# Half a tile more distance between the scores and what reads the probabilities back

## The reference, cut to what matters

```python
Q, K, V = (proj(Wq), proj(Wk), proj(Wv))
scores = jnp.einsum('bhqd,bhkd->bhqk', Q, K) / SCALE
idx = clip(k - q, -MAX_LEN, MAX_LEN) + MAX_LEN
scores = scores + jnp.einsum('bhqd,qkd->bhqk', Q, pek[idx]) / SCALE
scores = jnp.where(causal, scores, -jnp.inf)
attn = jax.nn.softmax(scores, axis=-1)
out = einsum('bhqk,bhkd->bhqd', attn, V) + einsum('bhqk,qkd->bhqd', attn, pev[idx])
x = _layernorm(x + out @ Wo.T)
x = _layernorm(x + (silu(x @ wg.T) * (x @ wu.T)) @ wd.T)
```

## Time and profile before

| | us |
|---|---|
| median of 3 runs | 5945.27 (5935.37 to 5958.6) |
| the profiled execution | 5937.08 |
| its span | 5935.4 |

### The profile page before, as it was taken

How to read it: one execution, slowest core, us unless ns; L and a number is a source line. 1 busy time by engine, 2 the same in 40 slices (tenths; PEclk the granted TensorE clock), 3 DMA queues, 4 the chain that set the end, 5 groups by cost and what they waited for, 6 DMA issues and landing times. The chain is left out here.

```text
span 5935.4 us, 143051 instructions
## 1 busy us (share of the span) xinstructions
PE 5156.7 (87%) x49460; PEld 3407.6 (57%) x49460; DVE 3809.4 (64%) x8777; ACT 3447.7 (58%) x7512; POOL 1838.5 (31%) x2516
## 2 busy tenths in 40 slices
PE   9977888888888888888888888888888799999999
PEld 5545555555555555555555555555555556666655
DVE  5546676676667766676667666776677645555554
ACT  4436777777777777777777777777677511111111
POOL 4443333333333333333333333333333211111111
PEclk9989999999999999999999999999999999999999
DMA  7888999999999999899999999899999711111111
GB/s 225 253 225 278 287 299 292 285 294 297 287 290 294 302 292 298 286 292 295 294 290 294 290 293 291 289 296 296 283 293 291 248 54 57 57 57 57 57 57 39
DMA packets 653784, 1417.28 MB, mean 239 GB/s; under 512 B 64004, under 2 KB 362088, under 8 KB 640872
## 3 DMA queue, kind: packets, MB, share of 16 engines
q1 hardware_dynamic: 653160, 1409.10, 75.7%
HBM read 737.46 MB, written 671.35 MB: 237 GB/s over the span
## 5 line engine op out<-in xcount | busy, mean ns | idle before, releaser
L791 ACT ACTIVATE a_prob<-a_neg_s,a_neg_max 128x384 f32<-128x384 f32 (+1 forms) x1792 | 1076.1, 601 | 275.1 <-DVE a_neg_max L840 255.8
L511 DVE COPY a_p_t<-a_t_ps 128x512 f32<-128x512 f32 (+3 forms) x1536 | 954.3, 621 | 258.5 <-PE a_t_ps L755 251.9
L688 PE MATMUL a_s_ps<-a_k,a_q 96*128 96x512 bf16 (+3 forms) x3072 | 860.1, 334 | 192.8 <-ACT a_far L795 178.2
L762 PE MATMUL a_t_ps<-a_ident,a_band 128*128 128x128 f32 x3840 | 630.6, 285 | 384.3 <-DMA a_band<-prob_scr 359.4
L798 ACT ACTIVATE a_b_out<-a_t_ps 128x512 f32<-128x512 f32 (+1 forms) x1024 | 582.2, 569 | 635.9 <-PE a_t_ps L698 632.7
L840 DVE CUSTOM_DVE_ANT_1 a_neg_s<-a_s_ps,a_bias,a_far_neg 128x384 f32<-128x384 f32 x1280 | 791.1, 618 | 237.3 <-DVE a_far_neg L834 237.3
L755 PE MATMUL a_t_ps<-a_ident,a_prob 128*128 128x128 f32 x5120 | 865.4, 276 | 0.2 <-DVE a_p_t L511 0.2
L834 DVE TENSOR_REDUCE a_far_neg<-a_s_ps 128x1 f32<-128x640 f32 (+4 forms) x1280 | 708.9, 554 | 220.5 <-PE a_s_ps L688 120.9
L716 PE MATMUL a_o_ps<-a_p_t,a_v 128*32 128x128 f32 x18432 | 832.1, 294 | 0.2 <-ACT a_o_t L803 0.2
L798 ACT ACTIVATE a_p_t<-a_t_ps 128x512 f32<-128x512 f32 (+3 forms) x1536 | 669.7, 436 | 155.2 <-PE a_t_ps L755 151.4
L795 ACT ACTIVATE a_far<-a_s_ps,a_neg_max 128x640 f32<-128x640 f32 (+4 forms) x1280 | 732.4, 572 | 0.0
(11 more groups left out here) (99 smaller groups left out, 6660.9 us busy)
## 6 DMA issues: line engine op xcount, KB each, us to landing
a_bias<-bias_scr SPq DMA_DIRECT2D x448, 576.0 KB, 6.2
prob_scr<-a_prob SPq DMA_DIRECT2D x448, 576.0 KB, 7.1
bias_scr<-a_b_out SPq DMA_DIRECT2D x448, 512.0 KB, 4.0
a_band<-prob_scr SPq DMA_DIRECT2D x448, 512.0 KB, 6.1
qk_scr<-p_parts SPq DMA_DIRECT2D x256, 192.0 KB, 3.4
v_scr<-p_v_out SPq DMA_DIRECT2D x256, 128.0 KB, 2.2
a_v<-v_scr SPq DMA_DIRECT2D x64, 512.0 KB, 7.0
attn_scr<-a_o_t SPq DMA_DIRECT2D x512, 64.0 KB, 6.4
```

Of the source, the lines that this page charges most:

```text
L511: copy(p_t[par][:, u, blocks[0] * P:(blocks[-1] + 1) * P], bank[:, 0:len(blocks) * P]) \
L688: mm = pe.matmul(s_ps[:, u % 2, c:e], q_s[0:ROWS, g, u, qb * P:(qb + 1) * P], k_s[0:ROWS, g, u, c:e], start=True, stop=True)
L762: mm = pe.transpose(bank[:, n * P:(n + 1) * P], band_block(kk, 2 * i + n // 2, n % 2), ident[:, :])
L791: e = act.activation(near_prob(k, u, near(qb)), neg_s[:, u % 2, 0:w].rearrange("p (b c) -> p b c", c=P), ACT.Exp, bias=neg_max[:, u:u + 1] ...
```

## The change

The transposes of the probabilities run six units behind the scores in place of four: in unit u of step k PE takes head (u - 6) mod 4 of tile k - 2 (units 0 and 1: heads 2 and 3) or k - 1 (units 2 and 3: heads 0 and 1). The band transposes, the three parts of the values and the relative values all run two units later as well, and ACT's copy to `o_t` with them. SP stores a tile's result a step later (in step k+4) and always waits for ACT's copy first. The loop has one more step at its very end.

```diff
-    DEPTH = 4
+    DEPTH = 5
...
-        BAND_SLOTS = ((3, 2), (0, 3))
-        VALUE_SLOTS = ((2, 2), (3, 2), (0, 3))
-        REL_SLOT = (1, 3)
+        P_LAG = 6
+        BAND_SLOTS = ((1, 3), (2, 3))
+        VALUE_SLOTS = ((0, 3), (1, 3), (2, 3))
+        REL_SLOT = (3, 3)
...
-                if ok(k - 1):
-                    jobs += [("p", u, k - 1, i) for i in range(len(t_banks(q_block(k - 1))))]
+                kp, head = k + (u - P_LAG) // GRP, (u - P_LAG) % GRP
+                if ok(kp):
+                    jobs += [("p", u, kp, i, head) for i in range(len(t_banks(q_block(kp))))]
...
-                    if k >= 0 and ok(k - 3):
-                        par = (k - 3) % 2
-                        qb, g = q_block(k - 3), ((k - 3) % TILES) // QB
-
-                        if not ok(k + LEAD):
-                            sp.wait_ge(o_evac, T - 2)
-                        row = attn[r_prev if k < 3 else r]
+                    if k >= 0 and ok(k - 4):
+                        par = k % 2
+                        qb, g = q_block(k - 4), ((k - 4) % TILES) // QB
+
+                        sp.wait_ge(o_evac, T - 3)
+                        row = attn[r_prev if k < 4 else r]
                         sp.dma_start(row[g, :, qb * P:(qb + 1) * P], o_t[:, par]).then_inc(stored[par], 16)
...
-                                pe.wait_ge(exp_ready, 4 * (TILES * r + kk) + u + 1)
+                                pe.wait_ge(exp_ready, 4 * (TILES * r + kk) + head + 1)
...
-                        if (u, 3) == REL_SLOT and ok(k - 3) and k >= 0:
+                        if u == REL_SLOT[0] and ok(k - 3) and k >= 0:
                             relative(r, k - 3)
...
-                        if u == 1 and ok(k - 3) and k >= 0:
+                        if u == REL_SLOT[0] and ok(k - 3) and k >= 0:
                             act.wait_ge(o_mm, T - 2)
                             if ok(k - 5):
                                 act.wait_ge(stored[(k - 3) % 2], pair(r, k - 5))
```

More of the change, by code:

```diff
@@ L462, in plan @@
                 if ok(k + LEAD) and u in BIAS_SLOTS:
-                    jobs.append(("bias", u, k + LEAD, BIAS_SLOTS.index(u)))
-                if ok(k - 1):
-                    jobs += [("p", u, k - 1, i) for i in range(len(t_banks(q_block(k - 1))))]
+                    jobs.append(("bias", u, k + LEAD, BIAS_SLOTS.index(u), None))
+                kp, head = k + (u - P_LAG) // GRP, (u - P_LAG) % GRP
+                if ok(kp):
+                    jobs += [("p", u, kp, i, head) for i in range(len(t_banks(q_block(kp))))]
                 for i, (at, back) in enumerate(BAND_SLOTS):
                     if u == at and ok(k - back):
-                        jobs.append(("band", u, k - back, i))
+                        jobs.append(("band", u, k - back, i, None))
             return jobs
@@ L480, in wait_evac @@
         def wait_evac(eng, r, job):
-            kind, u, kk, i = job
+            kind, _, kk, i, head = job
             if kind == "band":
@@ L485, in wait_evac @@
             elif kind == "p":
-                who = t_engine(q_block(kk), u, i)
-                eng.wait_ge(t_evac[who], t_done(who, r, kk, u, i))
+                who = t_engine(q_block(kk), head, i)
+                eng.wait_ge(t_evac[who], t_done(who, r, kk, head, i))
             else:
@@ L499, in read_out @@
         def read_out(eng, copy, name, r, k, u, first, last):
-            for pos, (kind, uu, kk, i) in enumerate(plan(k, first, last)):
+            for pos, (kind, uu, kk, i, head) in enumerate(plan(k, first, last)):
                 if uu != u:
@@ L505, in read_out @@
                 by_head = bank.rearrange("p (h j) -> p h j", h=2)[:, :, j:]
-                if kind == "p" and t_engine(q_block(kk), u, i) == name:
+                if kind == "p" and t_engine(q_block(kk), head, i) == name:
                     blocks = t_banks(q_block(kk))[i]
-                    eng.wait_ge(t_mm, t_made(r, kk, u) - len(t_banks(q_block(kk))) + i + 1)
+                    eng.wait_ge(t_mm, t_made(r, kk, head) - len(t_banks(q_block(kk))) + i + 1)
                     if valid(kk - 2, first, last):
                         eng.wait_ge(pv_mm, TILES * r + kk - 1)
-                    copy(p_t[par][:, u, blocks[0] * P:(blocks[-1] + 1) * P], bank[:, 0:len(blocks) * P]) \
+                    copy(p_t[par][:, head, blocks[0] * P:(blocks[-1] + 1) * P], bank[:, 0:len(blocks) * P]) \
                         .then_inc(t_evac[name], 1)
@@ L742, in body @@
                         for pos, job in enumerate(jobs):
-                            kind, uu, kk, i = job
+                            kind, uu, kk, i, head = job
                             if uu != u:
@@ L752, in body @@
                             elif kind == "p":
-                                pe.wait_ge(exp_ready, 4 * (TILES * r + kk) + u + 1)
+                                pe.wait_ge(exp_ready, 4 * (TILES * r + kk) + head + 1)
                                 for n, b in enumerate(t_banks(q_block(kk))[i]):
                                     mm = pe.transpose(bank[:, n * P:(n + 1) * P],
-                                                      prob_block(kk, u, b), ident[:, :])
+                                                      prob_block(kk, head, b), ident[:, :])
                                 mm.then_inc(t_mm, 1)
```

## The result

| | before | changed |
|---|---|---|
| median of the runs | 5951.9 us (4 runs) | 5699.5 us (4 runs: 5692.3 to 5712.8) |
| ratio | 1 | 0.957 (95% interval 0.9551 to 0.9589) |
| span of the profiled execution | 5935.4 us | 5690.6 us |

The changed kernel takes 252 us less. The forecast was 5800 us with a range of 5670 to 5930, so the direction and the range hold, and the gain was taken too small (141 us). The time is nearer to that of rival A (5670 us) than to that of the forecast.

A forecast was written before the change was run, and what follows sets the result against it. Nothing full, PE 85% and DMA 93% busy; PE's band wait held back stores and loads. Per round 2.7 - 0.4 - 0.1 = 2.2 us, x 64 = 141; 5937.1 - 141 + 3 gave 5800 us, range 5670 to 5930.

The forecast's parts named there:

- rival A: Attention stage: nearly all comes back, DMA runs full, new store wait does not show; 4.2 us a round, 5670 us; chance 0.20.
- The bands: PE's wait for the `a_band` load before band transposes goes altogether; gain at most 5.6 us a round, or 358 us.
- What comes back: Part of the band wait regained per round, limited by DMA: between 0 and 4.7 us, taken as 2.7 us.
- floor: Round length at a full DMA share of 1.00: 66.6 x 0.93 = 61.9 us, a gain of 4.7 us.
- The relative-key chain: `a_bias` load and POOL's selects before DVE: 7.7 us, up to 10.1; holds the DMA share at 0.97.
- The store: ACT's copy of a result tile waits for an earlier store to land: 0 to 1.9 us a round, taken as 0.4.
- The banks: A step's last transposes and the next relative keys share a bank; PE waits for ACT's copy, 0.1 us a round.
- The copies: DVE's heavy copies gather around heavy steps: 2.8 to 4.4 us a round, mostly hidden, taken as 0.
- rival C: DVE's heavy copies beside heavy steps are paid in full, 2.8 to 4.4 us a round; slower, 5995 us; chance 0.11.
- B: Band wait turns into DVE and ACT waits for `a_bias`; round shrinks within 0.3 us, 5918 to 5940 us; chance 0.12.
- D: Band transposes still wait, as SP's load comes later by its new wait; 5.6 us stay, 5935 us; chance 0.05.

The follow-up runs named there:

- e1: Kernel before, but PE's band transposes read a constant tile and wait for no load (relative values left out of the result): 5723.5 us, ratio 0.9604.
- e9: Kernel before, band transposes of a constant tile (relative values left out), three `a_bias` buffers and their earlier load: 5473.8 us, ratio 0.918.
- e4: Changed kernel, but POOL masks a constant tile without waiting for `a_bias` (relative-key scores left out of the result): 5607.7 us, ratio 0.9402.
- e7: Changed kernel with three `a_bias` buffers, SP loading `a_bias` before its wait for ACT's `b_out` copy: 5593.3 us, ratio 0.941.
- e10: Kernel before with three `a_bias` buffers and the earlier `a_bias` load, band wait kept: 5540.3 us, ratio 0.9298.
- e11: Changed kernel with three `a_bias` buffers, earlier `a_bias` load, and probability copies dealt out otherwise between DVE and ACT: 5546.1 us, ratio 0.9302.
- e2: The change at half its size: everything one unit later than in the kernel before instead of two: 5941.2 us, ratio 0.997.
- e5: e2 with four result buffers (`a_o_t`) in place of two: 5857.3 us, ratio 0.9858.
- e3: Changed kernel with the three banks handed out by a count running on over the steps: 5707.0 us, ratio 0.9566.
- e12: e5 with the three banks handed out by a count running on over the steps: 5866.2 us, ratio 0.9837.

## Why the prediction was right, and where its sizes were off

**The bands: right.** 5.6 us a round were put down as the wait that goes; it went (1.0 us in 2000 left), and e1 shows that this wait is the cause of 92% of the gain. SP's new wait for the earlier band's transposes costs next to nothing, as said: 2.9 us in 2000. One reading was loose. SP does not wait for the `b_out` copy before it issues anything of the step: the band load and the store of the probabilities come first in its program, and what the late copy holds back is L582, L593 and all behind them, the next step's band load included. One sign did not come out either: steps of over 11 us became rare, but four are left.

**What comes back: the mis-sized term.** I took 2.7 us a round, from a DMA share of 0.97; measured are 3.8 us with a share of 0.96. The share came out as forecast and the round did not, since the busy time (round times share) is no constant: 66.6 x 0.93 = 61.9 us of it in a round before, 62.8 x 0.96 = 60.3 us after, 59.4 x 0.99 = 58.8 us in e9, with the same bytes. The "floor" of 61.9 us was none: e4, e7, e9, e10 and e11 all run below it. The window of e9, as an example:

```profile
2000.00:4000.00 2000.00, 1841.35 (x23319) 1269.40 (x23317) 1542.68 (x3907) 1630.62 (x3636) 780.26 (x911) 0.99 0.99 328
```

Its last two numbers are a share of 0.99 and 328 GB/s. The page "DMA: Bandwidth & Descriptors" (Specifications) of the Trainium skill, with its 358 GB/s, was the better bound: no run here reaches its figure over these 2000 us (a window of 4 us did, 379 GB/s in the earlier trace rows), while mine was passed by five. For this change alone my share was nearer: 2.7 us a round, where the page's bound would have given back the whole 5.6, against 3.8 measured.

**The relative-key chain: right as the next limit.** It was named with 7.7 us, up to 10.1, and e4 and e7 put its price at 1.6 to 1.7% of the time before. But ACT's 117.8 us, which I read as its sign, are for the most part something else: ACT waits 85.2 us for DVE's maxima in e7 as well, where DVE waits for no relative keys.

```profile
ACT a_prob L795 <- DVE a_neg_max L844: 85.2, 288, 0.7
```

**The store: right in kind.** 0.4 us a round were taken, 4.3 us in 2000 is 0.14. e2 shows that it is no fancy: a unit less, and it makes 71.9 us of waiting on ACT in 2000, 2.4 us a round, of which e5 got 1.3 back. The diff also has SP wait for ACT's copy before each of these stores, for which the sum has no term:

```profile
SPq L613 <- ACT a_o_t L804: 44.5, 67, 1.3
```

SP stands 44.5 us in 2000 there, with the next band load behind it. Whether that costs time no run shows.

**The banks: right to be small.** In front of the relative keys PE waits 0.9 us in 2000 for ACT's copies and 9.9 for DVE's (10.5 before). PE's new wait is for DVE's copies in front of the probabilities, 43.0 us in 2000; it belongs to the copies, for without the shared bank it is still there (e3).

**The copies: taken at 0, with a cost that does not show while the relative-key chain is there.** Against e1, which has the old order, the change is not slower. When that chain no longer holds DVE up, the new order costs 1.8 us a round (e9 against e7). The other deal of copies gets back 0.7 of them (e11); that the rest is due to the copies too is not shown. The 2.8 to 4.4 us of rival C were an upper end that no run reaches.

**Rivals.** A gave 5670 us and came nearest, in part by luck: DMA did not run full in the change (0.96), and A's round of 62.4 us came from the floor that was none. B is excluded by the time, though a part of what it says happened: DVE waits 38 us more in 2000 for `a_bias`. D is excluded by the trace. C has a part of its mechanism, not its outcome.

## What to carry to other kernels

A wait for a transfer can be hidden by distance or made shorter where the transfers are issued, and the two are not alike: distance costs order and buffers everywhere between, and here the issuing side (one load in the queue behind a wait that it did not need; the third buffer and the earlier place came together) gave more, 0.9298 against 0.957. Before moving consumers away from a late load, look what its transfers share the queue with, and what the issuing engine stands waiting for while it could issue. When distance is moved, check each buffer that a later point now holds longer: a half-sized move was held up in part by the result's store, which no view of the kernel before showed as a wait.

The best kernels measured here are e10 and e11, equal within their intervals; e10 needs no change of order.

## What the runs showed of the hardware that was not expected

The DMA busy share is not a gauge of what is left: at 0.93 the stage moved 293 GB/s in the kernel before (296 and 298 in e12 and e5), at 0.96 310, at 0.97 319 and 322, at 0.99 328, and with 10.2% fewer bytes 285 at 0.91. The busy time for the same bytes (round times share) fell by 5% from the slowest to the fastest kernel. Landing times differ between kernels that issue the same transfers at other moments: the store of the probabilities, 576 KB, took 7.1 us in the median before, 6.9 in the change, and 4.8 in e7, with the same transfers around it in number and size.

```profile
prob_scr<-a_prob SPq DMA_DIRECT2D x229, 576.0 KB, 4.8
```
